# Two long attentions of a four-stage image kernel, issued in another order

## What is computed

```
# stage 0, per image: 8 heads of 16 channels, 1024 places
q, k, v = split(qkv_w @ x + qkv_b)
out = x + proj_w @ softmax(q^T k * 128**-0.5) v + proj_b
# stage 2, per image, on normalized x: 8 heads of 16 channels and 2 of 64
standard = softmax(qh kh^T / 4) vh                     # 8 heads
multi_i  = softmax(qm_i km_i^T / 8) vm_i               # 2 heads of 64, q from the gated x
fused    = silu([standard, multi] @ ff_w1.T + b1) @ ff_w2.T + ...
```

## Time and profile before

| | |
|---|---|
| median of three runs | 4891.36 us (4887.98 to 4895.34) |
| profiled execution, own time | 4894.81 us |
| its span | 4893.0 us |
| TensorE matmul busy | 4230.3 us (86%) |
| VectorE busy | 3664.8 us (75%) |
| ScalarE busy | 3122.5 us (64%) |
| GpSimd busy | 1554.2 us (32%) |
| VectorE, maxima of the second attention (L664, `c_mx`) | 1529.6 us in 1280, 1222 ns each |
| VectorE, maxima of the first (L664, `a_mx`) | 1217.2 us in 1024, 1221 ns each |
| ScalarE, exponentials (L562), second and first | 1388.1 and 1110.9 us |

### The profile page before, as it was taken

The page is one execution under the profiler, slowest core; times in us unless marked ns, Lnnn a source line. Parts: engine busy times, 40 slices in busy tenths (PEclk is TensorE's granted clock), DMA queues, the critical chain, the costliest instruction groups (busy, mean ns, idle before and its releaser), DMA issues. The chain is left out here.

```text
span 4893.0 us, 69363 instructions
## 1 busy us (share of the span) xinstructions
PE 4230.3 (86%) x25808; PEld 1221.5 (25%) x25808; DVE 3664.8 (75%) x4203; ACT 3122.5 (64%) x5565; POOL 1554.2 (32%) x862
## 2 busy tenths in 40 slices
PE   3999989999996767399999999999999999678888
PEld 1212122122112633122222222222222222123332
DVE  5999999999993347677777777777777777277774
ACT  1888888888886235177776667676777667334443
POOL 1011111011000023143334444444433443346666
PEclk6999999999998988599999999999999999889999
DMA  2222313213211124211111111111111110111211
GB/s 59 57 45 60 64 45 72 52 45 73 54 40 49 61 96 168 55 38 47 45 45 47 47 44 33 38 32 47 47 47 45 45 39 17 40 57 65 75 54 55
DMA packets 144278, 261.91 MB, mean 54 GB/s; under 512 B 58192, under 2 KB 58192, under 8 KB 143824
## 3 DMA queue, kind: packets, MB, share of 16 engines
q1 hardware_dynamic: 143952, 257.61, 20.1%
HBM read 155.13 MB, written 85.13 MB: 49 GB/s over the span
## 5 line engine op out<-in xcount | busy, mean ns | idle before, releaser
L664 DVE TENSOR_REDUCE c_mx<-banks 128x2 f32<-128x1024 f32 x1280 | 1529.6, 1222 | 479.4 <-PE banks L470 302.8
L562 ACT ACTIVATE c_e<-banks 128x512 f32<-128x512 f32 x2560 | 1388.1, 594 | 655.0 <-PE banks L496 330.8
L664 DVE TENSOR_REDUCE a_mx<-banks 128x2 f32<-128x1024 f32 x1024 | 1217.2, 1221 | 140.1 <-PE banks L462 130.0
L562 ACT ACTIVATE a_e<-banks 128x512 f32<-128x512 f32 x2048 | 1110.9, 594 | 223.7 <-PE banks L486 203.2
L511 PE MATMUL banks<-a_e,a_vs 128*32 128x512 f32 x4096 | 560.9, 620 | 0.2 <-ACT a_e L562 0.2
L511 PE MATMUL banks<-c_e,c_vs 128*32 128x512 f32 x4096 | 546.3, 605 | 0.0
L409 POOL TENSOR_TENSOR c_esum<-c_e,c_esum 128x1024 f32<-128x1024 f32 x224 | 527.1, 2353 | 42.8 <-ACT c_e L562 21.9
L462 PE MATMUL banks<-a_stack 48*128 48x512 f16 x2048 | 389.4, 397 | 91.8 <-DVE a_mx L664 48.7
L462 PE MATMUL banks<-c_stack 48*128 48x512 f16 x2048 | 385.1, 393 | 92.9 <-DVE c_mx L664 69.0
L486 PE MATMUL banks<-a_stack 50*128 50x512 f16 x2048 | 405.8, 393 | 53.2 <-ACT a_e L562 49.4
L486 PE MATMUL banks<-c_stack 50*128 50x512 f16 x2048 | 398.5, 386 | 25.2 <-ACT c_e L562 17.2
(11 more groups left out here) (320 smaller groups left out, 4627.6 us busy)
## 6 DMA issues: line engine op xcount, KB each, us to landing
a_stack<-q_halves SPq DMA_DIRECT2D x96, 128.0 KB, 3.6
a_stack<-k_halves SPq DMA_DIRECT2D x96, 128.0 KB, 6.8
c_stack<-q_halves SPq DMA_DIRECT2D x96, 128.0 KB, 4.6
c_stack<-k_halves SPq DMA_DIRECT2D x96, 128.0 KB, 6.4
a_res<-in_x SPq DMA_DIRECT2D x16, 512.0 KB, 4.0
a_xin<-in_x SPq DMA_DIRECT2D x16, 512.0 KB, 4.5
q_halves<-a_parts SPq DMA_DIRECT2D x16, 512.0 KB, 3.0
k_halves<-a_parts SPq DMA_DIRECT2D x16, 512.0 KB, 2.8
```

Of the source, the lines that this page charges most:

```text
L562: nc.scalar.activation(e[q % 4][:, 2 * i + h, :], bank_of(n - 1 + h), ACT.Exp).then_inc(st_free, 1)
L664: nc.vector.tensor_reduce(mx[j % 2][:, :, i, qc, half], slot[:, :, :], AX.X, ALU.max).then_inc(mr_free, 1)
```

## The change

`timetable` alone is changed; all instructions stay, and the other lines move down by six. The fixed offsets are replaced by a table, `PLACES`, with one row for each attention.

```
+PLACES = {
+    False: dict(score=0.12, values=0.13, evac=0.50, score2=0.60, maxima=(0.62, 0.99), lead=(3.0, 3.0), lowest=0.86, turn=1.48,
+                load=-19.4, reach=-15.96, bound=-4.74, qk=(-3.04, -2.27, -0.19, 2.66), v=(1.75, 2.73), proj=(15.99, 17.54)),
+    True: dict(score=0.01, values=0.12, evac=0.13, score2=0.14, rate=(1.79, 1.95, 1.41), lead=(5.35, 4.59, 7.74), lowest=0.17, turn=0.72,
+               load=-26.48, reach=-44.42, bound=-21.92, qk=(-20.62, -17.56, 1.31, 1.34), v=(5.02, 12.31), dqk=(0.36, 4.41, 5.28, 9.56),
+               dsum=11.93, proj=(25.58, 31.69))}
...
-            maxima = first - SLOTS - LEAD
...
+            until = first - place["lead"][g]
+            for i in range(16 * group.twos):
+                if mixed:
+                    when = until - (16 * group.twos - i) / place["rate"][g]
                 else:
-                    add(maxima + i + MAXIMA, "pair", b, g, 0, i // 2, i % 2)
-            add(first - LEAD - 1 + 0.95, "lowest", b, g)
-            add(first - LEAD + 0.70, "turn", b, g)
+                    when = until - SLOTS + i // 2 + place["maxima"][i % 2]
+                add(when, "pair", b, g, i // 16, i % 16 // 2, i % 2)
+            add(until + place["lowest"], "lowest", b, g)
+            add(until + place["turn"], "turn", b, g)
```

More of the change, by code:

```diff
@@ L90, in timetable @@
         ahead = start - size
-        piece = lambda slot, *step: add(slot + PIECE, *step)
-        add(ahead - size + begin + 12.5 if mixed else ahead - size + 4.5, "load", b)
+        add(ahead + place["load"], "load", b)
         if b == 0 or not mixed:
[L94 to L97, removed]
+            add(ahead + place["reach"], "reach", b)
+            add(ahead + place["bound"], "bound", b)
+            add(ahead + place["bound"] + 0.01, "ratio", b)
+            add(ahead + place["bound"] + 0.80, "scales", b)
@@ L98, in timetable @@
         for i in range(4):
-            piece(ahead + begin + i, "qk", b, i // 2, i % 2)
-        add(ahead + begin + 3.95, "split", b)
-        add(ahead + begin + 6.5, "stackstore", b)
+            add(ahead + place["qk"][i], "qk", b, i // 2, i % 2)
+        made = ahead + place["qk"][3]
+        add(made + 0.25, "split", b)
+        add(made + 2.80, "stackstore", b)
         for i in range(6):
-            add(ahead + begin + 8.5 + i, "stackload", b, i)
+            add(made + 4.80 + i, "stackload", b, i)
@@ L104, in timetable @@
         for i in range(2):
-            piece(ahead + (begin + 4 + i * 2 if mixed else 2 + i), "v", b, i)
+            add(ahead + place["v"][i], "v", b, i)
         if mixed:
             for i in range(4):
-                piece(ahead + begin + 8 + i, "dqk", b, i // 2, i % 2)
-            add(ahead + begin + 12, "dsplit", b)
+                add(ahead + place["dqk"][i], "dqk", b, i // 2, i % 2)
+            add(ahead + place["dqk"][3] + 0.30, "dsplit", b)
         for g, group in enumerate(groups):
@@ L123, in timetable @@
                     slot = first + KC * half + kc
-                    add(slot + SCORE, "score", b, g, half, kc, 0)
+                    add(slot + place["score"], "score", b, g, half, kc, 0)
                     if group.kind == "S":
-                        add(slot + SCORE2, "score", b, g, half, kc, 1)
+                        add(slot + place["score2"], "score", b, g, half, kc, 1)
                     else:
-                        add(slot + SCORE + 0.01, "esum", b, g, half, kc)
-                    add(slot + 2 + VALUES, "pv", b, g, half, kc)
-                add(first + KC * (half + 1) + 1 + EVAC, "evac", b, g, half)
+                        add(slot + place["score"] + 0.01, "esum", b, g, half, kc)
+                    add(slot + 2 + place["values"], "pv", b, g, half, kc)
+                add(first + KC * (half + 1) + 1 + place["evac"], "evac", b, g, half)
             done = first + SLOTS + 2
             if group.kind == "D":
-                piece(done + 2, "dsum", b, g)
-                done += 3
+                add(first + SLOTS + place["dsum"], "dsum", b, g)
+                done = first + SLOTS + place["dsum"] + 0.3
             add(done, "sums", b, g)
@@ L142, in timetable @@
                 add(done + 4.7, "norm", b, g)
-        done = start + size + (13 if mixed else 9)
         for i in range(2):
-            piece(done + 2 * i, "proj", b, i)
-        add(done + 3.9, "store", b)
-        add(done + 3.9, "residual", b + 1)
+            add(start + size + place["proj"][i], "proj", b, i)
+        add(start + size + place["proj"][1] + 1.9, "store", b)
+        add(start + size + place["proj"][1] + 1.9, "residual", b + 1)
     return [step for _, _, step in sorted(at)]
```

7 lines of the change are left out of this document (1 added, 6 removed).

## The result

The changed kernel takes 4785.74 us (median of four runs, 4777.87 to 4789.99) against 4892.51 before: a ratio of 0.9781, 95% interval 0.9764 to 0.9798. The forecast was 4815, with a range of 4740 to 4885 and faster as the likely side. So side and range held, and the gain of 107 us was 31 larger than forecast. The profiled execution took 4782.51 us, its span is 4780.5.

What follows compares the result with a forecast made beforehand. No engine was full: ScalarE's exponentials and the score chain set 2.39 us slots, VectorE's reductions the second bound. First attention -41, second -40, its start +5 make -76 us: 4815, range 4740 to 4885.

Steps and rivals of the forecast that it cites:

- the walk over slots 13 to 18: First attention, new order: delays from `lowest`, `turn`, `reach` and both `proj` in these slots cost 3.1 us an image together.
- the lower clock: First attention, old order: the slot run at the lower granted clock after the wait at `bound` costs some 0.8 us.
- the 0.3 for slow landings: First attention: store and residual's load no longer go just ahead of the second group's rows, gaining 0.3 us an image.
- just enough: First attention, second group: `proj` and VectorE's delays stretch the time before the first score to 5 us, covering the later transposition.
- half of the old waits: D group of the second attention: half of the old waits were taken to stay, giving 39.5 us, -1.6 an image.
- The prediction's floor of 38.4: D group of the second attention: 16 slots with 29 pairs and a `turn` take 38.4 us with all VectorE waits gone.
- the split into pieces (+0.5) and VectorE's waits (-1.6): Second attention's S slots: moved pieces cost 15.6 instead of 15.1 us; VectorE's waits shrink from 2.2 to 0.6; net -1.1 per image.
- the 0.6 that was let stay: Second attention's S slots: of 2.2 us an image of waits for VectorE at pairs, 0.6 was assumed to remain.
- Only one attention gains: Rival, whole kernel: late rows in the first attention or TensorE's full slots in the second take the rest; 4855 us, chance 0.17.
- Covers are swapped: Rival, both attentions: pieces cost their length anywhere and new VectorE waits replace old ones; -5 to +5, 4890 us, chance 0.09.
- Pairs in the score's way: Slower rival, second attention: eleven pairs per image each wait 0.77 us for VectorE, holding up scores; 4951 us, chance 0.10.
- The stream closes up: Rival, both attentions: VectorE's reductions become the only clock, -6.2 and -4.4 us an image; 4737 us, chance 0.15.

Runs made afterwards that it cites:

- proj_early: The changed kernel with the first attention's two `proj` back in slots 9 and 11, the store and residual following them: 4809.7 us (0.9829).
- pairs_behind: The changed kernel with the second attention's eleven pairs per image between a score and `pv` or the second score moved right behind these: 4794.8 us (0.9810).
- second_only: The changed kernel with the first attention back in the old order, only the second in the new one: 4830.3 us (0.9874).

## Why the prediction was right, and where its sizes were off

**First attention (-2.7 an image forecast, -3.7 measured).** The new order's terms held: the walk over slots 13 to 18 was 3.1, the table gives 0.52 + 1.09 + 1.66 = 3.3; `bound` and `scales` 0.45, slot 27 gives 0.3. Of the old order's terms, the wait at `bound` (2.6; slot 24 gives 2.5) and `turn` (1.1; 1.2) held too. The mis-sized term is the lower clock: 0.8 was taken from one stretch, but the old order's images without the dip take 88.7, so it costs 1.5 on average. Part of it stood under another name: the 0.3 for slow landings was the mean image over a quiet one of 89.8, and the images that take 89.8 have a dip too (the one that begins with the `bound` of the earlier trace rows takes 89.81); the landings cost before only 0.8 us in thirteen images. The two `proj` cost 0.82 + 1.09 = 1.9 and not 1.7. The rest (`v`, `qk`, the first group's `turn` and the late rows) was set at nothing and gained 0.3. The late transposition is hidden at the second group by the `proj` ("just enough" was right, as `proj_early` shows) in eleven of thirteen images; in the two others TensorE waits 0.6 and 1.3 us for the rows, over the 0.5 named as a limit. The longer of the two is again a slow landing (669.91 to 673.23), with no store and no residual's load issued in the 30 us before it, so the prediction's reason for slow landings is at least not the only one. The first group's rows, for which 0.5 an image was charged, make TensorE wait twice, 0.3 us in all.

**Second attention (-2.7 forecast, -4.2 measured).** All of the difference is the D group, 39.5 forecast and 38.0 measured. The step that failed is "half of the old waits" stay. `pairs_behind` divides the gain: the new rate and lead alone (29 pairs in the group instead of 32, the `turn`'s slot 2.89 instead of 3.98) bring the group from 41.1 to 39.3, the seven pairs ahead of `pv` bring it on to 38.0. These had been entered as a danger. The prediction's floor of 38.4 was also too high: with the waits gone 37.55 was reached. It counts 16 whole slots, but the group as it is measured begins behind the first slot's `c_dparts` (0.66 us, 2768.98 to 2769.64 in after), and 38.4 - 0.66 is 37.7.

**S slots (-1.1 forecast, -1.0 measured).** The sum held, and so did the slots: 0.75 us over a clean slot in slot 0, 1.6 in slot 1, 2.7 in slot 5 (5.06 us; "some 5 us" was named), 2.1 in slot 12. But the split into pieces (+0.5) and VectorE's waits (-1.6) did not. They are no two terms: moved alone, each makes the S slots longer (1.7 and 4.4). Nor is the 0.6 that was let stay a wait: no wait for VectorE is left in the list, and the 0.66 of the D group's first `c_dparts`, which the S slots as measured include, stands in its place. So a walk through the new order slot by slot found the right length of the pieces; that the total came out to 0.1 is in part luck, and its bookkeeping by cause was wrong.

**Starts.** +5 was forecast for the second attention's, and +2.3 measured between these two profiles. It varies: from `bound` to the first score it takes 74.9 to 77.5 us in the three profiles with the old stream of pairs and 77.9 to 80.1 in the eleven with the new one. The first attention's start, -4.0, had no term; 2.6 of it appear without the change too.

**The rivals.** *Only one attention gains* is refuted by the two kernels with one each. *Covers are swapped*: in part true of the first attention (`reach` and `proj` moved waits rather than removed them, 0.5 and 0.2), not of the whole. *Pairs in the score's way*: the sign was wrong in the D group (-1.3 from these pairs) and right, with 0.6 us an image for its four pairs in place of 0.77 each, in the S slots. *The stream closes up* came near in the second attention (it had -4.4 there, -4.2 was measured) and went half the way in the first (-6.2 and -3.7), where VectorE is busy 1060.85 of 1124.20 us, 94% against 91% before. The Trainium skill ("Perfetto Trace Analysis", Identifying the Most-Contended Engine), cited there, reads occupancy as a fair measure of nearness to the limit for VectorE; by it a third of the room was taken. That TensorE's busy share does not tell this, the same section says, and the trace agrees: 37.89 of 37.98 us in the D group, and yet the same instructions fit into 37.55.

## What to carry to other kernels

Walk a new order slot by slot against the engine that holds each slot, and don't give its gain to one of two moves before each has been run alone: here either half of the change alone made the S slots longer, and both together made them shorter. Two steps that need the same two buffers did better on the two sides of a long step of the engine that issues them than behind each other; this is shown for the D slots here, where each takes VectorE 1.2 us to drain. A wait that looks covered may still be dear through the clock, so price it from several images, not from one.

## What the runs showed of the hardware that was not expected

The granted clock is not a property of the order alone. With the same instructions in the same order, the 10 us around TensorE's wait at `bound` had a granted clock of 1.00, 0.83 or 0.66, and the image took from 88.7 to 91.1 us. The clock fell there in twelve of thirteen images of before and in four of thirteen of `second_only`, whose first attention is the same. The Trainium skill ("TensorE: Matmul & The Clock Gate", Part 1) says that the number of slow matmuls at a kernel's start differs between runs of one kernel. The trace shows something near it, not the same: in the middle of a run, the fall comes and goes from image to image.

At the end of the first attention, with TensorE busy some 7 of 10 us and no pairs left, the clock fell to 1.2 GHz in one kernel and held in another that differs by the place of two `proj` steps: 25 us. ScalarE, which had paced the slots, was then the one that waited (5.9 of 10 us busy instead of 8.2). What made it fall is not shown.
